# A memset and a wait for its signal between the gathers of a one-core graph and expert kernel

## What is computed

```python
def reference(x, src, dst, ...):
    # graph layer, on LN(x); src are the rows summed into
    agg = segment_sum(x[dst], src, num_segments=6250)
    h = agg + x
    h = (h @ W1 + b1) @ W2 + b2
    # expert layer, on LN(x)
    w = softmax(mean(x, axis=0) @ Wr + br)            # [rows, 8]
    h = relu(bn1(einsum('bfd,edh->bfeh', x, W1) + b1))
    h = relu(bn2(einsum('bfeh,ehk->bfek', h, W2) + b2))
    y = einsum('bfeh,ehd->bfed', h, Wo) + bo
    return einsum('bfed,fe->bfd', y, w)
# x = x + graph(LN(x)); x = x + expert(LN(x))
```

## Time and profile before

| | |
|---|---|
| median of 3 runs | 1381.97 us (1381.46 to 1383.72) |
| profiled execution, span from the first to the last instruction | 1595.0 us |
| time around the span of the profiled execution | not given |
| PE busy | 1279.8 us, 80% of the span |
| DVE busy | 1197.4 us, 75% |
| ACT busy | 868.3 us, 54% |
| POOL busy | 805.0 us, 50% |
| gathers (L544) | 830, from 235.8 to 1497.0 us |

### The profile page before, as it was taken

One profiled execution on the slowest core, in us unless ns is written; L12 is line 12 of the kernel. 1 busy time (PEld: TensorE's weight loads), 2 busy tenths in 40 slices (PEclk: granted clock), 3 DMA queues, 4 the chain that ended last, 5 costly groups with the idle time before them and its releaser, 6 DMA issues.

```text
span 1595.0 us, 25908 instructions
## 1 busy us (share of the span) xinstructions
PE 1279.8 (80%) x8179; PEld 841.9 (53%) x8179; DVE 1197.4 (75%) x3476; ACT 868.3 (54%) x1623; POOL 805.0 (50%) x864
## 2 busy tenths in 40 slices
PE   3868885557687778888878878898888998788998
PEld 3746652345454445455545545554555666565665
DVE  9999985566667666777777877777778887777865
ACT  7887451344455435454445544555545665555685
POOL 3000006666556666666666666666666556656300
PEclk9969997778799988999999999999999999999999
DMA  9301135333232332333333333343333323332200
GB/s 292 99 0 53 54 100 170 109 98 103 83 103 86 110 91 87 111 88 100 102 89 113 87 90 113 87 116 87 89 111 88 107 83 107 88 105 86 74 11 11
DMA packets 82235, 150.86 MB, mean 95 GB/s; under 512 B 16855, under 2 KB 55034, under 8 KB 82100
## 3 DMA queue, kind: packets, MB, share of 16 engines
q0 software_dynamic: 39840, 108.84, 23.8%
q1 hardware_dynamic: 42260, 40.36, 8.0%
HBM read 129.87 MB, written 19.27 MB: 94 GB/s over the span
## 4 chain that ended last, share of the span: by engine, by line
PE 47%; DVE 24%; issue 12%; another core or an unknown queue 8%; ACT 7%; DVEq 2%; ACTq 0%
PE PA L1555 11%; PE PB L1571 11%; DVE acc L1071 5%; PE PL L1589 4%; DVE zz L837 4%; PE PT L1589 4%; PE PN L1589 3%; DVE zz L838 3%; DVE onehot L1002 2%; DVE xt L1190 2%; ACT PB L742 2%; PE PN L1505 2%; PE PT L1505 1%; PE PT L1504 1%
## 5 line engine op out<-in xcount | busy, mean ns | idle before, releaser
L544 POOL DMA_INDIRECT gbuf<-xn_hilo,dsti x830 | 790.3, 952 | 667.5 <-issue 196.8
L741 ACT ACTIVATE h<-PB,bnt,bns 128x512 f16<-128x512 f32 (+3 forms) x240 | 167.7, 699 | 325.9 <-remote 177.5
L1555 PE MATMUL PA<-yT,wsplit 128*128 128x512 f16 (+3 forms) x1440 | 318.1, 361 | 13.0 <-issue 9.4
L1571 PE MATMUL PB<-h,wsplit 128*128 128x512 f16 (+3 forms) x1440 | 300.3, 347 | 5.6 <-issue 5.6
L730 ACT ACTIVATE h<-PA,bnt,bns 128x512 f16<-128x512 f32 (+3 forms) x240 | 167.8, 699 | 215.8 <-remote 104.2
L1555 PEld LDWEIGHTS PA<-yT,wsplit 128*128 128x128 f16 x1440 | 143.3, 103 | 114.9 <-issue 31.3
L1173 DVE TENSOR_TENSOR h<-PB,h 128x512 f16<-128x512 f32 (+3 forms) x240 | 139.9, 587 | 84.8 <-ACT PB L742 64.5
L1571 PEld LDWEIGHTS PB<-h,wsplit 128*128 128x128 f16 x1440 | 141.2, 101 | 98.3 <-issue 13.0
L1002 DVE TENSOR_SCALAR onehot<-iota_row,srel 128x128 f16<-128x128 f16 x830 | 178.2, 267 | 0.0
L1167 DVE TENSOR_TENSOR h<-PA,h 128x512 f16<-128x512 f32 (+3 forms) x240 | 139.5, 587 | 40.2 <-ACT PA L731 31.8
L1071 DVE TENSOR_TENSOR acc<-acc,PN 128x256 f32 x276 | 114.0, 413 | 71.9 <-issue 23.8
(11 more groups left out here) (250 smaller groups left out, 1856.5 us busy)
## 6 DMA issues: line engine op xcount, KB each, us to landing
gbuf<-xn_hilo,dsti POOLq DMA_INDIRECT x830
xt<-x_whole_bins SPq DMA_DIRECT2D x49, 128.0 KB
out<-xt SPq DMA_DIRECT2D x49, 128.0 KB
acc<-in_x SPq DMA_DIRECT2D x4, 1536.0 KB
x_whole_bins<-acc SPq DMA_DIRECT2D x4, 1536.0 KB, 11.8
xn_hilo<-xt SPq DMA_DIRECT2D x24, 256.0 KB, 2.1
h<-in_L_ffn_W SPq DMA_DIRECT2D x9, 256.0 KB, 4.3
zz<-in_L_ffn_W SPq DMA_DIRECT2D x5, 256.0 KB
```

What stands on the lines that cost most here:

```text
L544: pool.indirect_dma_start(gbuf[:, k % SLOTS, :], None, xn_dram, bass.IndirectOffsetOnAxis(dsti[:, k:k + 1], 0)).then_inc(gat[k % SLOTS], 16)
L741: nc.scalar.activation(h2[:, e % 2, 0, h, 0:w], PB[:, h, 0:w], ACT.Relu, bias=sh, scale=sc)
L1555: last = T_.matmul(PA[:, h, 0:w], wsp[0][:, e, k, wp, h * P:(h + 1) * P], yT[:, g % 2, yp, k, 0:w], start=n == 0, stop=n == 5)
L1571: last = T_.matmul(PB[:, h, 0:w], wsp[1][:, e, k, wp, h * P:(h + 1) * P], h1[:, e % 2, yp, k, 0:w], start=n == 0, stop=n == 5)
```

## The change

Before every gather from `k = 19` on (k > 18), POOL clears columns 400 to 655 of `junk` on all 128 partitions, 256 halves per partition. The memset raises a new semaphore, `paced`, by one, and POOL waits until `paced` has reached `k - 18`, that is for this very memset. Nothing else in the program changes; three lines more shift the line numbers behind L543.

```diff
             "bo_done", "bo_added", "l1_done", "l2_done", "l3_done", "z1_ready", "z2_ready", "lo1_ready", "lo2_ready",
-            "y3_added", "out0", "out1", "ord_ready", "mem0")}
+            "y3_added", "paced", "out0", "out1", "ord_ready", "mem0")}
...
                 if k >= SLOTS and k % 2 == 0:
                     pool.wait_ge(s["ent_done"], k // 2 - RING + 1)
+                if k > SLOTS:
+                    pool.memset(junk[:, 400:656], 0.0).then_inc(s["paced"], 1)
+                    pool.wait_ge(s["paced"], k - SLOTS)
                 pool.indirect_dma_start(gbuf[:, k % SLOTS, :], None, xn_dram,
                                         bass.IndirectOffsetOnAxis(dsti[:, k:k + 1], 0)).then_inc(gat[k % SLOTS], 16)
```

## The result

| | before | with the change |
|---|---|---|
| median of the runs, us | 1382.68 (1381.46 to 1383.72, 4 runs) | 1613.57 (1613.01 to 1615.01, 4 runs) |
| ratio | | 1.167, 95% interval 1.166 to 1.169 |
| span of the profiled execution, us | 1595.0 | 1611.4 |

A forecast was written before the change was run, and what follows sets the result against it. Before the change gathers were taken to set no time; with it POOL becomes the bound. Pace 1.25 + 0.26 + 0.09 = 1.60 us, time 297 + 811 x pace, 1595 us, range 1420 to 1700.

The forecast's parts named there:

- POOL is the bound after the change, PE waits at L1504: Gather loop: at 1.60 us a gather POOL exceeds the others' need, so PE finds the ring empty.
- The need of the other engines, 1.526 us in the trace and 1.32 in the runs: Before the change, the time per gather that engines other than POOL set, above POOL's own pace of 1.25 us.
- The reserve of 275 us in the trace's time: POOL's waits for PE and "remote" before the change, 188 entries, taken as its spare time in the first profile.
- The ends scaled by 0.866: Stretches before the first gather and behind the last, shortened to runs' time: 235.8 to 204.2 and 78.4 to 67.9 us.
- The memset, 0.26: Added memset of 256 halves on POOL: 0.26 us, the middle of 0.20 by bytes and 0.31 by elements.
- The wait, 0.09: POOL's wait for the memset's signal before the next gather: 0.09 us, from chained POOL steps at the start.
- the gap kept at 0.30: The 0.30 us "issue" gap between POOL's gathers stays once, in full, beside the memset and the wait.
- POOL keeps its pace with and without load on the others: Gathers on POOL alone stay 1.25 us apart in unprofiled runs, while PE, DVE and ACT times scale by 0.866.
- The rival of the shrunk pace: POOL's pace shrinks with the rest when nothing is recorded: 1.60 x 0.866 = 1.386, time 1421 us; chance 0.18.
- The start distance as the price of a memset: Memset priced by distance between starts, 0.19 us, not by its record: pace 1.53, time 1538 us; chance 0.15.
- The hidden memset: Memset and wait fit inside POOL's 0.30 us gap between gathers: pace 1.25, time 1382 us; chance 0.08.
- The faster rival: Memsets spread the gathers, so DVE's one-hots collide less and shorten: some 4 us saved, 1378 us; chance 0.02.

The follow-up runs named there:

- five variants: Edits of the changed kernel: memset of 2 halves 1447.9 us, odd gathers only 1497.9, no wait behind 1524.5, 128 floats 1531.4, 512 halves 1785.6.
- the second profile: The kernel before, unedited, profiled again: span 1380.6 us, runs' median 1381.8 us, ratio 1.000.

## Why the prediction was right, and where not

- **POOL is the bound after the change, PE waits at L1504: right and shown**, by the chain, by PE's waits and by five variants that each moved POOL's pace and the time with it. That it *becomes* the bound holds only behind about entry 640; before that it was one already.
- **The need of the other engines, 1.526 us in the trace and 1.32 in the runs: wrong.** The step took rows of the first profile and scaled them by 0.866. In the second profile gathers are 1.26 us apart before the change, and without half of the gathers the kernel takes 48 us less, with PE at 1.19 us an entry up to entry 618 and 1.33 behind it. So POOL had no reserve for most of the stretch. The statement that before the change the gathers set no time was wrong. The doubt was at hand: 1382 - 259 - 78 = 1045 us for 811 gathers is 1.29 each, next to the 1.25 of POOL alone. The reserve of 275 us in the trace's time was also summed wrong: it holds the usual 0.30 us gap of its 188 waits, 56 us, without which it is 219, as 811 x 0.27 gives too.
- **The ends scaled by 0.866: wrong.** They took 259.0 us to gather 18 and 80.7 from the last gather, near the unscaled 259.4 and 81.0 of the first trace. With 1.8 us around the span the constant was 342 and not 297, 45 us too little.
- **The memset, 0.26: too small**, it took 0.33. By elements was the right end of the two (0.31), by bytes the wrong one (0.20).
- **The wait, 0.09, and the gap kept at 0.30: together 0.39, measured 0.27.** The gap of 0.30 does not stay beside a memset: 0.16 of it is left, and the wait adds 0.105. Memset, wait and gap together came to 0.60 where the sum had 0.65; the pace was 1.548, mean 1.568 with the irregular rounds, for which the sum had no term, instead of 1.60, 26 us too much.
- The two errors of size, +26 and -45 us, in part cancel: 1595 + 45 - 26 = 1614. That the time was hit within 19 us is owed to this, and so is in part luck.
- **POOL keeps its pace with and without load on the others: right.** The rival of the shrunk pace (1421) is out, for in the runs the distance is 1.25, too. The start distance as the price of a memset is not refuted by these runs: its 0.19, the middle of 0.14 and 0.24, is what the memset costs without the wait, and its 0.28 with the wait is nearer to the measured 1.548 - 1.251 = 0.30 than the 0.35 of the forecast. Its time of 1538 missed mainly by the same 45 us in the constant; with 342 it would be 1583, 31 us too little, where the forecast would be 1640, 26 too much. What speaks for the completion is that a waiting gather starts 0.27 us behind the end of the record at all four sizes; but from 128 to 256 floats record and start distance grow by nearly the same (0.10 to 0.11 and 0.10 us), so the sizes do not tell the two apart. The hidden memset (1382) is out as a whole and right in a part, for 0.14 us of the gap give way to the memset. The faster rival is out: it had the one-hots grow shorter, and with the memsets they grew longer (last section).
- **The range** held. The pace of 1.50 to 1.73 was bounded well from both sides; with the constant of 342 it would have meant 1559 to 1745.
- **Of what would show it**: no waits of POOL for PE and a lead of 3 us came, distances of 1.55 to 1.57 are near the 1.60, and the memset's 0.33 lay just above its 0.31. The span near 1640 did not come (1611): its ends were right, and the pace was 26 us too much. Its nearness to the old span of 1595 says nothing, since that span was not the kernel's usual one.

## What to carry to other kernels

Compare the span of a profile with the median of the runs before any row is used; where they differ by 15%, as here, profile again before scaling: one factor for the whole hid that only one stretch had been slow. POOL, which issues the gathers, was the bound for most entries at a busy share of 59%: divide the stretch by the number of its transfers and set that beside their start distance where nothing is waited for. And a reserve that a ring shows late is worth nothing to a delay put early: ask of a delay at which point of the program the waiting changes sides.

## What the runs showed of the hardware

- In these runs a GpSimd memset costs by elements, 0.8 ns each over some 0.11 us, for halves as for floats (0.11, 0.22, 0.33, 0.54 us for 2 halves, 128 floats, 256 and 512 halves).
- Between two gathers that wait for nothing lie 0.30 us. With a memset between that nobody waits for, 0.16 follow it, and 0.27 if the gather waits for its signal.
- The memsets stretch DVE's one-hots (L1002, now L1005) while the shortest stay at 0.24 us. Duration min/median/max with 256 and with 512 halves, against 241/247/496 in the earlier trace rows and a median of 250 in the second profile:

```profile
L1005 DVE TENSOR_SCALAR onehot<-iota_row,srel x830: 241/286/633, 236.8 to 1507.6; 128x128 f16<-128x128 f16 x166
```

```profile
L1005 DVE TENSOR_SCALAR onehot<-iota_row,srel x830: 242/518/814, 236.8 to 1676.4; 128x128 f16<-128x128 f16 x166
```

The memset's own record stays at 0.325 us in median and 0.405 at most, so it is DVE that waits. The longest one-hots, 0.63 and 0.81 us, are 0.24 plus a little more than a whole memset of 0.33 or 0.54. The Trainium skill, SBUF — State Buffer, Who interferes with whom, says that GpSimd and a DVE instruction in a two-port mode exclude each other for the whole instruction; the stretched one-hots agree with it, though no run shows in which mode they are. The gathers stretch some of them too, which a median hides: in the second profile of the kernel before the mean is 275 ns, 150 of the 830 take over 300 and up to 507, and every one of those runs beside a gather's record, while the 34 that meet none take 252 at most. With the change the mean is 320, some 37 us more of DVE's work over 830 one-hots. These runs show no time lost by it, for with memsets before every gather POOL waits for no other engine, and its pace sets PE's.
